# A GRU scan with a routed feed-forward layer: side work of the first nine steps shared anew, three turns put behind a unit

## The reference, cut to what matters

```python
def cell(h, x):
    gi = x @ W_ih + b_ih
    gh = h @ W_hh + b_hh
    i_r, i_z, i_n = jnp.split(gi, 3, axis=-1)
    h_r, h_z, h_n = jnp.split(gh, 3, axis=-1)
    r = jax.nn.sigmoid(i_r + h_r)
    z = jax.nn.sigmoid(i_z + h_z)
    n = jnp.tanh(i_n + r * h_n)
    h_new = (1.0 - z) * n + z * h
...
topk_p, topk_idx = jax.lax.top_k(probs, TOPK)          # 4 of 128 experts
basis = jax.nn.silu(gate) * up                         # 8 blocks of 128 columns
mixed = jnp.einsum('tek,tki->tei', mix_sel, basis)
down = jnp.einsum('tei,ih->teh', mixed, w_down)
out = jnp.einsum('teh,te->th', down, coeff)
shared = jax.nn.silu(xt @ shared_w_gate) * (xt @ shared_w_up) @ shared_w_down
x = x + out + shared
```

## Time and profile before

| what | us |
|---|---|
| median of 3 runs | 145.73 |
| lowest, highest | 145.5, 149.58 |
| the profiled execution, its own time | 146.3 |
| span of its records | 144.4 |
| PE busy | 136.0 (94%) |
| DVE busy | 104.5 (72%) |
| ACT busy | 72.8 (50%) |
| POOL busy | 67.9 (47%) |

### The profile page before, as it was taken

One profiled execution on the slowest core, in us unless ns is written; L12 is line 12 of the kernel. 1 busy time (PEld: TensorE's weight loads), 2 busy tenths in 40 slices (PEclk: granted clock), 3 DMA queues, 4 the chain that ended last, 5 costly groups with the idle time before them and its releaser, 6 DMA issues.

```text
span 144.4 us, 4045 instructions
## 1 busy us (share of the span) xinstructions
PE 136.0 (94%) x1489; PEld 98.3 (68%) x1489; DVE 104.5 (72%) x388; ACT 72.8 (50%) x246; POOL 67.9 (47%) x123
## 2 busy tenths in 40 slices
PE   7999999999899999999999999999999999899981
PEld 5556677666466667767676767676767676688881
DVE  2206699999878887785878587768785878676661
ACT  0404764666746575455545554555455535433830
POOL 2301165666656455435544554455445544884030
PEclk9999999999999999999999999999999999999999
DMA  3986995000000000000100010001000100010102
GB/s 78 310 272 181 289 339 156 2 7 0 0 5 0 0 0 5 2 2 5 36 0 0 5 36 0 7 2 36 5 0 0 36 5 0 2 36 0 36 5 73
DMA packets 5859, 7.12 MB, mean 49 GB/s; under 512 B 976, under 2 KB 4304, under 8 KB 5840
## 3 DMA queue, kind: packets, MB, share of 16 engines
q1 hardware_dynamic: 5616, 6.83, 14.7%
q10 hardware_dynamic: 224, 0.04, 0.1%
HBM read 5.81 MB, written 1.05 MB: 48 GB/s over the span
## 4 chain that ended last, share of the span: by engine, by line
PE 71%; DVE 14%; DMA 5%; ACT 4%; issue 3%; SPq 2%; DVEq 0%
PE unit L640 36%; PE gates L619 14%; PE down L702 5%; PE gates L583 5%; DMA whh<-in_L_cond_W_hh_dram 5%; DVE wlo L899 3%; DVE early L853 2%; PE route L652 2%; ACT sc_add L423 2%; DVE sc_out L879 2%; PE turned L690 1%; DVE pre L870 1%; PE route L675 1%; PE unit L598 1%; DVE hT L886 1%
## 5 line engine op out<-in xcount | busy, mean ns | idle before, releaser
L304 POOL CAST hThi<-hT 128x64 fp32r<-128x64 f32 x32 | 10.7, 333 | 56.2 <-DVE hT L886 56.2
L640 PE MATMUL unit<-whi,hThi 128*128 128x512 f32 x80 | 34.2, 427 | 0.1
L640 PE MATMUL unit<-wlo,hThi 128*128 128x512 f32 x80 | 31.7, 396 | 0.0
L640 PE MATMUL unit<-whi,hTlo 128*128 128x512 f32 x80 | 31.5, 394 | 0.0
L619 PE MATMUL gates<-whh,hT 128*32 128x192 f32 x512 | 27.4, 332 | 1.6 <-DVE hT L886 1.2
L416 ACT ACTIVATE trz<-gates 128x128 f32<-128x128 f32 x32 | 8.8, 275 | 31.2 <-PE gates L619 31.2
L619 PEld LDWEIGHTS gates<-whh,hT 128*32 128x32 f32 x512 | 13.4, 109 | 11.6 <-issue 4.6
L879 DVE TENSOR_TENSOR_SCAN sc_out<-sc_mul,sc_add 128x128 f32<-128x128 f32 x32 | 13.8, 431 | 8.0 <-ACT sc_add L423 7.5
L640 PEld LDWEIGHTS unit<-whi,hThi 128*128 128x128 f32 x80 | 15.4, 192 | 5.0 <-issue 2.1
L640 PEld LDWEIGHTS unit<-wlo,hThi 128*128 128x128 f32 x80 | 15.0, 188 | 3.5
L927 DVE SCALAR_TENSOR_TENSOR p<-th,unit 128x256 f32<-128x256 f32 x40 | 15.9, 410 | 1.5 <-ACT th L444 1.5
(11 more groups left out here) (129 smaller groups left out, 239.1 us busy)
## 6 DMA issues: line engine op xcount, KB each, us to landing
xtok<-in_x_dram SPq DMA_DIRECT2D x8, 128.0 KB, 3.3
wraw<-in_L_ffn_w_gate_dram SPq DMA_DIRECT2D x2, 512.0 KB, 5.9
wraw<-in_L_ffn_w_up_dram SPq DMA_DIRECT2D x2, 512.0 KB, 6.9
out_dram<-ot SPq DMA_DIRECT2D x8, 128.0 KB, 2.1
wih<-in_L_cond_W_ih_dram SPq DMA_DIRECT2D x2, 384.0 KB, 4.1
whh<-in_L_cond_W_hh_dram SPq DMA_DIRECT2D x1, 512.0 KB, 6.7
whh<-in_L_cond_W_hh_dram SPq DMA_DIRECT2D x1, 256.0 KB, 5.3
wraw<-L_ffn_shared_w_gate_dram SPq DMA_DIRECT2D x1, 256.0 KB, 7.5
```

The costliest lines, as they stand in the source:

```text
L304: pool.tensor_copy(hThi[:, c % 3, :, :, k], hT[:, c % 2, :, k, :]).then_inc(hThi_ready, 1)
L640: last = pe.matmul(dst, st[:, p % 3, s, :, :].rearrange("p b t -> p (b t)"), w[:, s, :, cols], start=(s == 0 and n == 0), stop=(s == KB - ...
```

## The change

Four tables and two orders change; no arithmetic does.
- All three pairs of turned x are copied by ACT: pair 2 in step 1 as before, pair 4 in step 3, pair 6 in step 4. PE turns pair 4 in step 3 instead of 2, and pair 6 in step 4 instead of 3. DVE's `keep_x_pair` goes, and PE's waits for x go by `x_pair_turned`.
- High pieces: ACT writes piece 2 in step 3 and piece 3 in step 4 (before: two pieces in each), then two in each of the steps 5, 6 and 7. `hi_down` follows in step 8 instead of 7.
- Low pieces: DVE keeps three (3, 5, 7 in the steps 5, 6, 7) instead of four (2, 4, 5, 8 in the steps 3 to 6). POOL has seven instead of six, one in each of the steps 2 to 8; `lo_down` comes in step 9 instead of 8.
- In the steps with k = 3 `turn_hidden(p - 1)` stands behind unit 4 instead of ahead of it.

```diff
-TURN_PAIR = {1: 2, 2: 4, 3: 6}
-KEEP_PAIR_SCALAR = {1: 2}
-KEEP_PAIR_VECTOR = {2: 4, 3: 6}
-HI_AT = [(0, 0), (0, 0), (0, 2), (2, 4), (4, 6), (6, 8), (8, 10)]
-LO_VECTOR_AT = [[], [], [], [2], [4], [5], [8]]
-LO_POOL_AT = [[], [], [0], [1], [3], [6], [7], [9]]
+TURN_PAIR = {1: 2, 3: 4, 4: 6}
+KEEP_PAIR_SCALAR = {1: 2, 3: 4, 4: 6}
+HI_AT = [(0, 0), (0, 0), (0, 2), (2, 3), (3, 4), (4, 6), (6, 8), (8, 10)]
+LO_VECTOR_AT = [[], [], [], [], [], [3], [5], [7]]
+LO_POOL_AT = [[], [], [0], [1], [2], [4], [6], [8], [9]]
...
                 if c < 2:
                     pe.wait_ge(x_turned, c + 1)
-                elif c < 4:
-                    pe.wait_ge(x_pair_turned, 1)
                 else:
-                    pe.wait_ge(x_turned, c // 2 + 1)
+                    pe.wait_ge(x_pair_turned, c // 2)
...
                     if k == 0 and p == 0:
-                        pe.wait_ge(x_turned, 4)
+                        pe.wait_ge(x_pair_turned, 3)
...
                     if k == 3:
+                        unit(NU * p + 4, range(KB))
                         if p >= 1:
                             turn_hidden(p - 1)
-                        unit(NU * p + 4, range(KB))
...
-            def keep_x_pair(c):
-                dve.wait_ge(x_raised, c + 2)
-                dve.tensor_copy(xT[:, c:c + 2, :, :].rearrange("p c s (t b) -> p (c s) t b", t=TC),
-                                route[:, 0:4 * P].rearrange("p (a b t) -> p a t b", a=2 * KB, t=TC))\
-                    .then_inc(x_turned, 1)
-
...
-                if t in KEEP_PAIR_VECTOR:
-                    keep_x_pair(KEEP_PAIR_VECTOR[t])
```

## The result

The changed kernel took 149.07 us (median of 4 runs, 147.99 to 149.2), the kernel before 146.9 beside it (median of 4, now 145.5 to 149.58). The ratio was 1.0217, 95% interval 1.0186 to 1.0247: slower by 2.2%, and outside the range that I had given. As will be seen, that ratio sets late starts of the changed kernel against early starts of the kernel before; between runs that both start early it is 0.9982 (0.9960 to 1.0003).

A forecast was written before the change was run, and what follows sets the result against it. PE was taken as the bound from step 9 on, with the bound changing from step to step in steps 3 to 8. +1.06 at H(10) and -1.88 for the turns gave 145.73 - 0.82 = 144.9 us, range 143.6 to 146.6.

The forecast's parts named there:

- The last step, from the span to the time of runs: Whole run: span 143.6 plus 1.9 outside it gives 145.5; for the median of runs 145.73 - 0.82 = 144.9.
- POOL's longer step 9: POOL's high cast, 2.1 of `lo_down` and one scaling exceed step 9; the next steps were said to have room.
- rival F: Step 7: POOL's cast and low part of the state hold DVE, `em` 0.25 late, 145.15 in all; chance 0.1.
- Steps 2 to 6: PE keeps H(4) at 22.92 and sets H(5); DVE's relief buys little; H(8) 0.06 late, bounds -0.5 to +0.5.
- Rival D: Step 4 ends by the ring instead of PE, H(5) 0.5 sooner, and this lasts: 144.4; chance 0.08.
- Steps 7 and 8: ACT's two high pieces, then `hi_down`, make `emT` and H(9) 1.10 late, bounds 0 to 1.6; +1.06 at H(10).
- the wait for `emT`: Sign in step 8: PE's wait for ACT's `emT` grows from 0.35 to 1.2 to 1.5, with H(9) near 42.7.
- Rival C: Up to H(9): ACT's queue costs nothing and `emT` isn't late, only the turns' -1.88 counts: 143.85; chance 0.12.
- The turns: Behind unit 4, PE's wait for `mixed` goes: 0.25 at each of five loop places, 0.63 at the sixth, sum -1.88.
- Rival B: Idle ahead of the turns isn't a wait, so moving them saves nothing; ACT's queue at `emT` remains: 146.8; chance 0.15.
- Rival E: ACT's late copy of the turns holds the ring, 0.2 beyond the 0.35 cover in each of five steps: 145.9; chance 0.1.

The follow-up runs named there:

- tables alone: The changed kernel with the order of unit 4 and `turn_hidden` as before; ratio 1.0109 to the kernel before, 136.38 us from H(0) to the end.
- The later run: The changed kernel with `hi_down` in step 9 and `lo_down` in step 10, one step later each; runs 144.30 to 144.81 us, one 146.61.
- the best version: Kernel before plus turns behind unit 4, `hi_down` in step 10, low down pieces over steps 11 to 13, `WARM = 20`; median 143.59 us, ratio 0.9859.

## Why the prediction was wrong, point by point

The number and the range were wrong: 149.07 lies outside 143.6 to 146.6. Two steps failed, and they weigh very differently.

1. **The last step, from the span to the time of runs.** I took the stretch up to H(0) as given and the median 145.73 as the base. The three runs shown were 145.5, 145.73 and 149.58, and the last of them was no stray: ten of 25 runs of the kernel before had an early start and fifteen a late one, some 2 to 4 us apart. All of the four runs first taken of the changed kernel were late ones, near or above 148. That was bad luck, as six of its next 12 runs were early. It accounts for the miss: between runs with an early start the change measures -0.3 +- 0.3 us (0.9982), where -0.8 was predicted. The range should have had the second group in it, since 149.58 stood in the table.

2. **POOL's longer step 9, costed at nothing.** "The next steps have room" was right for POOL and forgot DVE: `lo_down` fell onto the scan of step 10, and the scaling behind it onto the halved state. Measured: 0.6 by H(12) (tables alone 43.16 against 41.32, with 1.28 of it by H(9)), gone when the block is split. I had seen this mechanism, as rival F, and looked for it only in step 8. There it showed as well, with 0.15 of the 0.25 that F gave it: the cast took 0.79, and `em` 0.44 instead of 0.29. The Trainium skill (SBUF — State Buffer, Who interferes with whom) has it that a VectorE instruction with two SBUF inputs and a GpSimd instruction that reads SBUF exclude each other, whichever was issued later waiting. The scan's 0.80 under `lo_down`, and 0.42 without, agree with it for VectorE as the one that waits.

3. **Steps 2 to 6.** Right. PE set H(4) and H(5), and relief of DVE bought nothing: step 4 took 4.26 (forecast 4.16), step 5 3.44, and H(8) came 0.06 late, as forecast. In between PE was later than forecast (0.47 at H(6) and 0.41 at H(7), where 0.27 and 0.2 stood), and the idle of step 7 took that up too. Rival D is out.

4. **Steps 7 and 8.** Right in mechanism, a little small: +1.10 at H(9) forecast, +1.24 to +1.28 measured; the longer `em` of rival F is about that excess. One sign missed: the wait for `emT` was 1.07 where 1.2 to 1.5 stood, since PE came to it 0.52 later itself, held by DVE ahead of unit 1. Step 9 gave back 0.09 (0.04 forecast), so H(10) is 1.15 late where 1.06 stood. The later run shows `hi_down`'s share alone as 0.75 (0.73 forecast). Rival C is out.

5. **The turns.** Right: -1.88 forecast; 132.54 against 134.37 is -1.83. In the loop each saved 0.25 to 0.26 (step 13: 3.36 instead of 3.62), of which steps beside them lost a few hundredths (1.16 in all at H(31)); the stretch behind H(31) is 0.67 shorter where 0.63 stood, and 0.70 in the changed kernel. Rival B is out. Rival E is out too: the copy on ACT ends 0.33 ahead of the tanh, where 0.35 was forecast.

Taken together, from H(0) to the end -0.82 was forecast, and -0.14 measured: 0.62 more for point 2 (H(10) to H(12)), 0.09 more for points 3 and 4 (up to H(10)), and 0.03 less for the turns (1.91 saved behind H(12), 1.88 forecast).

## What to carry to other kernels

Count times from an event behind the start (here the first step of the recurrence) before attributing a difference to an edit: a kernel whose only three runs lie at 145.5, 145.7 and 149.6 may have two starts, and neither a median of three nor a ratio of one group to the other is then a measure of the edit. An instruction that fills no gap of its own engine can still be late work for another: for each moved block write down the engine that queues behind it (ACT's `hi_down` ahead of `emT`) and the engine that shares its port (POOL's three in a row under DVE's scan). A small wait in a full pipeline is worth moving a consumer for: moving the turns saved 1.83 of the 2.77 that the best version saves from H(0) to the end (134.37 against 131.60).

## What the runs showed of the hardware that I had not expected

- TensorE rose from the pace of 1.2 GHz (256 columns in 0.21 us) to that of 2.4 GHz (0.11) at different moments in executions with the same instructions: at 4.4 in one and 6.6 in another with 30 unbroken matmuls, and with 13, followed by small matmuls with pauses, at 4.1 to 5.2 or only at 12.7 to 13.3. The clock column of the trace's windows read 1.00 in all of it, since it counts what lies ahead of the first clock record as full.
- A late rise costs 2 to 4 us in this kernel, at least as much as either part of the change; with seven more matmuls on zeros (1.5 us at the slow pace) none of 12 runs of two kernels started late.
- How far the transfer of the weights has come at a given step differs too: in four executions with H(0) at 9.16 to 9.56 ACT waited 0, 0.48, 0.74 and 2.02 for it in step 2, and only the last lost time by it (0.43 in step 3).
- A scan on DVE took 0.80 and 0.81 instead of 0.42 where POOL's subtractions were under way as it started, and a scaling of 64 columns on DVE 0.69 instead of 0.16 under POOL's scaling of 512.
